# Token weights first, x in two pieces, and seven broadcast stack transfers per image instead of twelve

## What is computed

```
def fake_quant(v):
    s = jnp.maximum(jnp.max(jnp.abs(v)), 1e-08) / QMAX
    return jnp.round(jnp.clip(v / s, -QMAX, QMAX)) * s
...
xq = fake_quant(x)
wq = fake_quant(w)
...
out = jnp.einsum('bcxpyq,dcpq->bxyd', xp, wq) + b
...
attn = jax.nn.softmax(jnp.einsum('bhqd,bhkd->bhqk', q, k) * scale, axis=-1)      # 12 heads of 16
x = jnp.einsum('bhqk,bhkd->bhqd', attn, v)
...
h = h + _L0_attn_ref(_layernorm(h, axis=-1), ...)
h = h + _L0_ffn_ref(_layernorm(h, axis=-1), ...)     # 16 experts of 768, the two best of each token
```

## Time and profile before

| what | value |
| --- | --- |
| three runs | 217.49, 217.42, 216.78 us; median 217.42 us |
| profiled execution: its time | 217.16 us |
| profiled execution: its span (first to last instruction) | 215.2 us |
| mean granted TensorE clock | 0.962 of full |
| busy: PE, weight loads, DVE, ACT, POOL | 178.3, 145.6, 121.5, 79.4, 65.7 us |
| chain that ended last, by engine | PE 58%, DVE 20%, DMA 7%, issue 6%, SP's queue 3%, ACT 3% |
| stack loads (L390) | 48 transfers of 73.5 KB, median 3.1 us from issue to landing |
| stores of the parts (L381) | 12 transfers of 147.0 KB, median 3.9 us |

### The profile page before, as it was taken

The page is one execution under the profiler, slowest core; times in us unless marked ns, Lnnn a source line. Parts: engine busy times, 40 slices in busy tenths (PEclk is TensorE's granted clock), DMA queues, the critical chain, the costliest instruction groups (busy, mean ns, idle before and its releaser), DMA issues.

```text
span 215.2 us, 5070 instructions
## 1 busy us (share of the span) xinstructions
PE 178.3 (83%) x1909; PEld 145.6 (68%) x1916; DVE 121.5 (56%) x396; ACT 79.4 (37%) x225; POOL 65.7 (31%) x82
## 2 busy tenths in 40 slices
PE   0098687989999988979699799899999999999710
PEld 0055574757577556456475699799999999989710
DVE  0488702673556868735276567754544656651454
ACT  2242532446654454455410533333533443335000
POOL 8902200000000100443503633177776721311100
PEclk9999999999999999999956999999999999999995
DMA  6996266866797789886520101999999935010073
GB/s 168 321 235 150 58 141 146 175 138 137 253 246 182 249 314 361 290 207 204 173 58 0 58 17 45 320 289 399 316 354 352 320 117 209 21 34 27 18 224 112
DMA packets 27270, 40.02 MB, mean 186 GB/s; under 512 B 8251, under 2 KB 21294, under 8 KB 27246
## 3 DMA queue, kind: packets, MB, share of 16 engines
q1 hardware_dynamic: 19790, 32.85, 51.0%
q10 hardware_dynamic: 5152, 4.05, 7.5%
q0 software_dynamic: 2304, 2.80, 4.0%
HBM read 30.50 MB, written 10.40 MB: 190 GB/s over the span
## 4 chain that ended last, share of the span: by engine, by line
PE 58%; DVE 20%; DMA 7%; issue 6%; SPq 3%; ACT 3%; POOL 2%; POOLq 0%; DVEq 0%; ACTq 0%
PE ps L1323 13%; PE ps L1331 13%; DVE mx L860 4%; PE ps L1209 4%; PE ps L1123 3%; PE ps L1179 3%; DMA wt_sb<-wtok 3%; PE ps L1155 3%; SPq L390 3%; PE ps L1079 3%; PE ps L1259 2%; PE ps L1229 2%; PE ps L1134 2%; DMA h<-halves_out 2%; PE ps L1193 2%
## 5 line engine op out<-in xcount | busy, mean ns | idle before, releaser
L683 ACT ACTIVATE hT<-ps,ring 128x128 f32<-128x128 f32 x96 | 26.5, 375 | 43.9 <-PE ps L1323 43.9
L860 DVE TENSOR_REDUCE mx<-ps 98x2 f32<-98x392 f32 x48 | 25.9, 564 | 21.4 <-PE ps L1209 21.2
L1323 PE MATMUL ps<-room,ring 64*128 64x128 f32 x612 | 37.4, 273 | 0.4 <-DVE room L923 0.4
L1323 PEld LDWEIGHTS ps<-room,ring 64*128 64x128 f32 x612 | 36.3, 188 | 0.9 <-issue 0.7
L1331 PE MATMUL ps<-ring,hT 64*128 64x192 f32 x384 | 35.0, 327 | 1.3 <-DVE room L991 0.8
L1331 PEld LDWEIGHTS ps<-ring,hT 64*128 64x128 f32 x384 | 31.1, 187 | 1.9 <-issue 0.9
L487 POOL TENSOR_TENSOR rstd<-var,power 98x2 f32<-98x2 f32 x8 | 5.6, 703 | 71.0 <-DVE var L756 71.0
L531 POOL DMA_INDIRECT halves_out<-room x15 | 15.0, 1001 | 29.1 <-DVE room L1042 27.6
L509 POOL DMA_INDIRECT slots<-rows,slotu x16 | 15.8, 985 | 13.3 <-DVE rows L802 4.6
L1209 PE MATMUL ps<-room 128*98 128x196 bf16 x96 | 16.1, 258 | 3.1 <-DMA room<-parts_out 1.4
L540 POOL DMA_INDIRECT slots<-rows,room x16 | 15.5, 969 | 5.1 <-issue 5.1
(11 more groups left out here) (175 smaller groups left out, 270.3 us busy)
## 6 DMA issues: line engine op xcount, KB each, us to landing
ring<-w SPq DMA_DIRECT2D x17, 579.0 KB, 5.5
ring<-w SPq DMA_DIRECT2D x17, 576.0 KB, 5.2
room<-parts_out SPq DMA_DIRECT2D x48, 73.5 KB, 3.1
parts_out<-parts SPq DMA_DIRECT2D x12, 147.0 KB, 3.9
ringb<-b SPq DMA_DIRECT2D x17, 96.0 KB, 6.7
slots<-padrow ACTq DMA_DIRECT2D x4, 388.0 KB, 10.8
halves_out<-padrow SPq DMA_DIRECT2D x1, 1176.0 KB
slots<-padrow ACTq DMA_DIRECT2D x1, 1164.0 KB, 13.5
```

Of the source, the lines that this page charges most:

```text
L683: nc.scalar.activation(hT[:, e % 2, m, :], hidden_block(e, m), ACT.Gelu, bias=ring2[:, e % RING, FC * D + m:FC * D + m + 1]).then_inc(gelu ...
L860: V.tensor_reduce(mx[:, i // 6, 2 * (i % 6):2 * (i % 6) + 2], ps[0:TP, n % 2, 0:2 * NQ].rearrange("p (h n) -> p h n", h=2), AX, ALU.max).t ...
L1323: last = mm(block(2 * pair + odd), ring1[rows, r, at:at + P], tokens[rows, k, :], start=(k == 0), stop=(k == 2))
```

## The change

**Head.** The token weights are the first transfer on SP's queue, and x follows in two transfers, columns 0 to 783 and 784 to 1567, each with a semaphore of its own. `amax` gets four columns. VectorE takes the weights' maximum, copies it into a second column, and takes a maximum of each half of x when that half has landed. TensorE turns columns 0 and 1 after the first half's maximum and columns 2 and 3 after the second's. The reduction to the scale then runs over 192 columns, not 96. VectorE's wait for the constants moves behind the maxima.

**Stacks.** The slots are dealt so that the copies of one part stand in neighbouring slots, and neighbouring slots are filled by one transfer whose source names the 16 rows twice or three times, with a leading dimension of step 0. Of the seven transfers of an image three fill one slot (16 partitions), three fill two (32 partitions) and one fills three (48 partitions). The products that are summed are the same six. Each image's transfers count on a semaphore of their own.

```diff
-STACK = (((0, 1, 2), (3, 4), (5,)), ((0, 3, 5), (1, 4), (2,)))
+STACK = ((((0, 2), (4, 5)), ((2, 4),), ((5, 6),)), (((3, 6),), ((1, 3),), ((0, 1),)))
+LOADS = sum(len(part) for side in STACK for part in side)
...
-            sp.dma_start(x_sb[0:KC, :], xp).then_inc(x_in, 16)
             sp.dma_start(wt_sb[:, :], wtok).then_inc(wt_in, 16)
+            for k in range(2):
+                sp.dma_start(x_sb[0:KC, TOK * k:TOK * (k + 1)], xp[:, TOK * k:TOK * (k + 1)]).then_inc(x_in[k], 16)
...
-                        for row in STACK[i][p]:
-                            sp.dma_start(stack[HD * row:HD * (row + 1), b % 3, :, :],
+                        for begin, end in STACK[i][p]:
+                            sp.dma_start(stack[HD * begin:HD * end, b % 3, :, :],
                                          parts_out[b, p, D * i:D * (i + 1), :].rearrange("(f h) n -> f h n", h=H)
-                                         ).then_inc(stack_in, 16)
+                                         .unsqueeze(0).to_broadcast([end - begin, HD, H, NQ])).then_inc(stack_in[b], 16)
...
-            dve.wait_ge(con_in, 16)
-
-            dve.wait_ge(wt_in, 16)
-            V.tensor_reduce(amax[:, 1:2], wt_sb[:, :], AX, ALU.max,
-                            apply_absolute_value=True).then_inc(amax_ready, 1)
-            dve.wait_ge(x_in, 16)
-            V.tensor_reduce(amax[:, 0:1], x_sb[0:KC, :], AX, ALU.max,
-                            apply_absolute_value=True).then_inc(amax_ready, 1)
-            dve.wait_ge(amax_turned, 1)
-            link(V.tensor_reduce(qs[:, 0:1], ps[0:2, 5, 0:KC], AX, ALU.max))
+            dve.wait_ge(wt_in, 16)
+            link(V.tensor_reduce(amax[:, 1:2], wt_sb[:, :], AX, ALU.max, apply_absolute_value=True))
+            V.tensor_copy(amax[:, 3:4], amax[:, 1:2]).then_inc(amax_ready, 1)
+            for k in range(2):
+                dve.wait_ge(x_in[k], 16)
+                V.tensor_reduce(amax[:, 2 * k:2 * k + 1], x_sb[0:KC, TOK * k:TOK * (k + 1)], AX, ALU.max,
+                                apply_absolute_value=True).then_inc(amax_ready, 1)
+            dve.wait_ge(con_in, 16)
+            dve.wait_ge(amax_turned, 2)
+            link(V.tensor_reduce(qs[:, 0:1], ps[0:2, 5, 0:2 * KC], AX, ALU.max))
...
-                        pe.wait_ge(stack_in, 16 * 12 * (b + 1))
+                        pe.wait_ge(stack_in[b], 16 * LOADS)
```

More of the change, by code:

```diff
@@ L148, in vit_block @@
         wtq = sb("wtq", [KC, 2, D], BF16)
-        amax = sb("amax", [KC, 2])
+        amax = sb("amax", [KC, 4])
         qs = sb("qs", [2, 4])
@@ L242, in vit_block @@
         ident = con[:, C_ID:C_ID + P]
-        con_in, x_in, wt_in, small_in, row_in, pad_in = (sem(n) for n in
-            ("con_in", "x_in", "wt_in", "small_in", "row_in", "pad_in"))
+        x_in = [sem(f"x_in{k}") for k in range(2)]
+        con_in, wt_in, small_in, row_in, pad_in = (sem(n) for n in
+            ("con_in", "wt_in", "small_in", "row_in", "pad_in"))
         ring_in = [sem(f"ring_in{i}") for i in range(RING)]
@@ L256, in vit_block @@
         var_ready, rstd_ready = sem("var_ready"), sem("rstd_ready")
-        part_ready, rest_ready, stack_in = sem("part_ready"), sem("rest_ready"), sem("stack_in")
+        part_ready, rest_ready = sem("part_ready"), sem("rest_ready")
+        stack_in = [sem(f"stack_in{b}") for b in range(IMG)]
         part_stored = [sem(f"part_stored{p}") for p in range(PARTS)]
@@ L1086, in _ @@
             pe.wait_ge(con_in, 16)
-            pe.wait_ge(amax_ready, 2)
-            tr(ps[0:2, 5, 0:KC], amax[:, :], ident[0:KC, 0:KC]).then_inc(amax_turned, 1)
+            for k in range(2):
+                pe.wait_ge(amax_ready, k + 2)
+                tr(ps[0:2, 5, KC * k:KC * (k + 1)], amax[:, 2 * k:2 * k + 2], ident[0:KC, 0:KC]).then_inc(amax_turned, 1)
             pe.wait_ge(scale_diag, 1)
```

## The result

The changed kernel takes **250.4 us** (median of four runs, 249.64 to 251.48), the kernel before 217.13 beside it: a ratio of 1.150 [1.145, 1.155], 33.3 us slower. The forecast was 240.0, with a range of 226 to 258. The sign, the mechanism and the image by image pattern came true. The saving in the head did not, and the stacks cost half as much again as forecast. Where the executions of a kernel spread by more than 1.5%, its ratio leaves out the slower ones, which flatters small gains, so these are given as medians of all executions too.

What follows compares the result with a forecast made beforehand. It saw the program's end hang on transfers in the head and in filling image 0's stacks. 217.16 us + 20.2 (image 3's lateness, head saving included) + 2.6 (clock) = 240.0 us, range 226 to 258.

Steps and rivals of the forecast that it cites:

- the mechanism: Stack loads with 2 or 3 copies outermost run on 2 or 3 engines, so they land late; chance above 0.80.
- the image by image pattern: First score matmuls of images 0 to 3 come 5.0, 10.5, 12.8 and 20.2 us late.
- The saving in the head: Start of the kernel: x in two transfers ends the maxima at 8.56 instead of 9.87 us, -1.2 us in all.
- the stacks: Stack loads take 14.8 us an image instead of 8.6, making image 3's first score matmul 20.2 us late.
- Who carries: Stack loads: engines follow the outermost dimension, so 32 rows run on 2 engines, 48 on 3, 16 rows to each.
- The price of a packet: Stack loads: 0.189 us per 4704-byte packet, 67 on the first engine, 12.7 us an image.
- the expert transfers: Image 3: expert transfers ahead of its stores hold engines 4.7 us; those ahead of its loads, with remaining stores, show 1.3.
- the prediction's last sign of being wrong: Stack loads: the forecast's size is wrong if the stores do not queue behind the loads.
- The step from image to image: Next image's stores stand behind the load packets, so its loads are issued 1.2 us later and each image adds delay.
- only image 0 pays: Rival: next images' stores pass the backlog, so only image 0's 5.0 us remain; 222 us, chance 0.03.
- The sum: Whole kernel: 217.16 + 20.2 + 2.6 = 240.0 us, with image 3's first score matmul at 94.3.
- The clock: After image 3's first score matmul: TensorE's idling lowers its granted clock, +2.6 us, between 0 and 5.1.

Runs made afterwards that it cites:

- e1: The kernel before with only the change's head edits, stacks keeping their twelve loads: 218.25 us against 217.33, ratio 1.004.
- e5: The changed kernel with the first eight expert weight loads and the zero fill held back until image 3's stack loads are issued: 256.41 us, 1.071 to the kernel before.
- e10: e5 again, on the third chip beside the changed kernel: 253.98 us, ratio 1.079 to the kernel before, 13.3 us less than the changed kernel.
- e7: The kernel before with nine stack loads an image, repeated k-side rows read with 2 or 3 parts outermost, no zero step: 254.12 us, ratio 1.064.
- e3: The kernel before with six stack loads an image, the 16 source rows as outermost dimension: 217.15 us, ratio 0.998.
- e2: The kernel before with only the change's seven stack loads an image, head as before: 248.22 us, ratio 1.139.
- e6: The kernel before with the change's seven loads for image 0 only, twelve for images 1 to 3: 248.89 us against 240.94, ratio 1.031.
- e4: The kernel before with the change's head and GpSimd's zeroing of `room` moved behind the four roots: 216.24 us against 217.33, ratio 0.990.
- e8: The kernel before with the change's head, zeroing behind the roots and six loads with 16 rows outermost: 239.28 us against 240.94, ratio 0.992.
- e11: The kernel before with only GpSimd's zeroing of `room` moved behind the four roots: 236.68 us against 236.17.
- e12: e8 again, on the third chip beside e11: 235.12 us against the kernel before's 236.17, ratio 0.993.

## Why the prediction was right, and where it was off

**The head: the step that failed.** The maxima did shorten (the last one ended at 8.2 us, forecast 8.56). What I left out is the engine that runs beside VectorE. The multiplication of the scales is held until the zeroing of `room` is over:

```profile
9.22 1.83 DVE L722 TENSOR_SCALAR qs<-con,qs 2x2 f32<-2x2 f32 x1
...
12.31 0.42 DVE L730 TENSOR_SCALAR wt_sb<-wt_sb,sc 96x384 f32<-96x384 f32 x1
```

It starts at 9.22, ends at 11.05, and the head gains 0 instead of 1.2. In the kernel before it ran from 10.83 to 11.06, so it already touched that end, unseen. In nine kernels it began under the zeroing, between 8.64 and 10.83 us, and ended at 11.04 to 11.06 every time, after 2.40, 2.19, 1.83, 1.62, 0.57, 0.47, 0.36, 0.36 and 0.23 us (e1, e5, the changed kernel, e10, e7, e3, e2, e6, the kernel before); with the zeroing moved it took 0.22 (e4, e8, e11, e12). The reduction and the one-column operation just before it ran at full speed under the same zeroing. That fits the Trainium skill, "SBUF — State Buffer", section "Who interferes with whom": a `tensor_scalar` can enter a mode that takes a port pair shared with GpSimd, a reduction cannot, and whoever comes second waits for the other's whole instruction. The traces show the waiting; which port it is they don't show.

**Who carries: right, to the packet.** The inference from 98, 128 and 16 rows held for 2 and 3, by the 57 reports an image above. In the stretch 40 to 43 us, in which image 0's loads move nearly alone, the queue's share of the 16 engines is two engines' share:

```profile
q1 hardware_dynamic: 42, 0.15, 12.5%
```

The rule of the Trainium skill ("DMA: Bandwidth & Descriptors", "Why a DMA increments its semaphore by 16 and not by 1"), which the prediction named beside that step, agrees with e3 and e7 as well. The advice of the Trainium skill, in the same page's section "Bandwidth", to batch transfers into larger ones was worth nothing here: six loads instead of twelve gave 0.998.

**The price of a packet: right when alone, too low beside the expert weights.** I took 0.189 us. From 84 to 88 us in e10, with nothing else moving, four microseconds carry 45 large packets on two engines (the 49 less the four small ones):

```profile
DMA packets 49, 0.21 MB, mean 53 GB/s; under 512 B 4, under 2 KB 4, under 8 KB 49
```

4 x 2/45 = 0.18 us. With 67 x 0.18 + 2.1 an image takes 14.2. Image 3 of e10 took 14.8.

For images 2 and 3 the rest is the expert weights: 19.6 us, and with them gone 15.9 and 14.8. The trace records the size of each packet, and those of 4704 bytes are the stacks'. From the 96th of an image's 192 packets to the end of the last passed 8.4, 8.5, 11.5 and 12.1 us in the changed kernel (images 0 to 3), and 8.4, 8.9, 8.7 and 8.3 in e10. From 92 to 98 us of the changed kernel, 42 stack packets started beside 276 of expert weights:

```profile
DMA packets 485, 1.56 MB, mean 260 GB/s; under 512 B 55, under 2 KB 167, under 8 KB 485
```

6 x 2/42 = 0.29 us each. Busy engines alone do not make them dear. From 100 to 104 us the engines are nearly as full (93.9% against 102.5%), but with the zero fill of `halves_out`, and 40 of the large packets are the stacks', 0.20 us each:

```profile
DMA packets 1390, 1.23 MB, mean 309 GB/s; under 512 B 28, under 2 KB 1342, under 8 KB 1390
```

I had counted the expert transfers only as time ahead of the loads (4.7 and 1.3 us) and never as a burden on packets already under way. Why the weights slow them while they move is not shown.

The next image's three stores stand where I had them, behind the load packets, on the two engines that carry the loads; on the engines that are free they pass. The DMA share and the packets of the changed kernel from 36 to 40 us (40 slices of 0.1 us) show one of them pass as a burst:

```profile
DMA  3032111112021111299998211202111111202111
DMA packets 416, 0.35 MB, mean 87 GB/s; under 512 B 371, under 2 KB 371, under 8 KB 416
```

416 - 371 = 45 large packets, as many as in the undisturbed 4 us of e10, so this burst took nothing from the loads. The last load packet ended at 43.01, and what follows from 43.1 to 44.9 us is small packets only, at the share of two engines:

```profile
DMA packets 135, 0.05 MB, mean 28 GB/s; under 512 B 135, under 2 KB 135, under 8 KB 135
q1 hardware_dynamic: 135, 0.05, 13.6%
```

After the start of the last load packet, 144 packets of 392 bytes start: 3 stores x 2 engines x 24 rows. So the prediction's last sign of being wrong, stores that do not queue behind the loads, did not come.

Images 0 and 1 took 2.0 and 0.8 us more than image 3 of e10, and spent them mostly before the 96th packet. In image 0 the first packet started 2.0 us after the first issue, in the other two 1.4. What held the early packets stays open.

**The step from image to image: right.** Each image was late by its own loads, e6 shows that image 0 alone costs 8.0 us, and the rival "only image 0 pays" is out. The loads' issue came 0.6 us after the release before it, not 1.2, and for image 3 5.2 us after it, forecast 5.9; without the expert transfers, 0.6.

**The sum.** At the first score matmul of image 3 the forecast was 94.3 and the trace says 104.7. The 10.4 us between are: head 1.2; image 0's loads 2.0 (16.8 instead of 14.8); image 1's 0.8; image 2's 4.8; image 3's 3.5 (19.6 instead of 16.1); less 0.6, 0.6 and 0.7 for earlier issues. So 8.3 of them are images 2 and 3. That 250.4 still lies in the range is partly luck: the range was drawn for the price of a packet alone, which was right, and its width took up a burden that it did not name and a saving that did not come.

**The clock.** From one of the four matmuls to the next the granted clock was 0.80, 0.85 and 0.78 in the changed kernel, where it had been 1.00 throughout. What follows that matmul is 249.5 - 104.75 = 144.75 us long, before 215.2 - 74.10 = 141.1: 3.65 us more, forecast 2.6. The windows (PE, PEld, DVE, ACT, POOL, then clock) of the changed kernel:

```profile
104.75:120.00 15.25, 13.89 (x133) 9.69 (x133) 10.49 (x40) 6.24 (x17) 0.43 (x2) 0.89 0.52 159
120.00:140.00 20.00, 16.56 (x164) 10.55 (x157) 8.99 (x40) 9.95 (x26) 9.77 (x12) 0.97 0.64 193
140.00:160.00 20.00, 18.35 (x108) 14.55 (x109) 12.93 (x71) 3.51 (x9) 6.16 (x10) 0.69 0.10 30
```

That is (0.11 x 15.25 + 0.03 x 20 + 0.31 x 20)/0.5 = 17 us at 1.2 GHz, where the kernel before had 10.2: 7 us more, worth at most 3.5. TensorE's busy time behind that matmul is 125.13 us against 121.95 before, 3.2 more for 1495 and 1493 matmuls. That the clock makes up the difference is worked out, not tested by a run of its own.

## What to carry to other kernels

Count a transfer's engines before its instructions: the outermost count of the pattern, not the number of rows, said how many carried it, and 67 packets in a row on one engine cost more than twelve issues on all sixteen. When a saving ends in a small instruction, look at what the neighbouring engine does at that moment, since an end that two things share moves only when both move. And price a packet twice, once alone and once with what the queue will hold beside it later in the program.

## What the runs showed of the hardware that I had not expected

- A VectorE multiplication of four numbers took 1.62 to 2.40 us instead of 0.22, ending with GpSimd's zeroing (e1, e5, e10, and the changed kernel).
- A store issued behind confined loads ran at once on the engines that they left free, and its packets for their two engines came after theirs. SP paid: the three stores of image 3 kept it 10.88 us (2.20 before), and one issue alone took up to 6.25.

```profile
L385 SPq DMA_DIRECT2D parts_out<-parts x12: 359/386/6249, 23.1 to 75.8; - x12
```

- The same kernel took 217, 236 and 241 us on three chips. The expert stage differs, not attention: in the slices of the page behind the middle e8 moves mostly 180 to 290 GB/s, where the earlier trace rows has seven slices in a row of 289 to 399. The mean granted clock is lower there too, 0.916 in e8's profiled execution against 0.962. Why these chips feed it less was not looked into.
